# Where the stores of kept orders stand between the two stages of a transform-and-attention kernel

## The reference

```
coeff = complex(x[..., 0], x[..., 1]) * sqrt_eig
h = irfft(einsum('nlm,mlk->nkm', coeff, pct), n=512, norm='forward')   # 64 x 256 x 512
z = layernorm(h)
logits = tanh(einsum(z @ K, z) + bias) * temperature, within a band of 12 of 256 rows
h = h + softmax(logits) @ z
h = h + ffn(layernorm(h))      # seven small layers on the few rows whose two marks are set
```

## Time and profile before

| | |
|---|---|
| median of three executions | 1432.56 us (1427.76 to 1433.67) |
| profiled execution | 1427.68 us |
| its span, first to last instruction | 1425.8 us |
| TensorE busy | 1335.9 us, 94% |
| VectorE, ScalarE, GpSimd busy | 65%, 63%, 39% |
| granted TensorE clock, mean over the span | 0.981 |
| bytes moved by DMA | 219.71 MB, mean 154 GB/s |

### The profile page before, as it was taken

One profiled execution on the slowest core, in us unless ns is written; L12 is line 12 of the kernel. 1 busy time (PEld: TensorE's weight loads), 2 busy tenths in 40 slices (PEclk: granted clock), 3 DMA queues, 4 the chain that ended last, 5 costly groups with the idle time before them and its releaser, 6 DMA issues. The chain is left out here.

```text
span 1425.8 us, 30434 instructions
## 1 busy us (share of the span) xinstructions
PE 1335.9 (94%) x8813; PEld 1159.2 (81%) x8813; DVE 928.9 (65%) x2026; ACT 899.8 (63%) x1956; POOL 557.0 (39%) x1394
## 2 busy tenths in 40 slices
PE   6989788969899999999999999999999989999994
PEld 4767566759799999999999999999999989555551
DVE  1222222326687887878888788887888877767772
ACT  1222222325577777777777777777777767867772
POOL 0000000000355555555555555555555546622222
PEclk9999999999999999999999999999999999999997
DMA  9999999995563333333333333333333332100000
GB/s 375 423 423 424 425 426 424 424 361 162 177 152 76 95 86 82 95 78 96 86 82 87 81 99 86 82 85 83 100 80 87 86 102 48 47 12 9 9 4 5
DMA packets 88338, 219.71 MB, mean 154 GB/s; under 512 B 20805, under 2 KB 33745, under 8 KB 75921
## 3 DMA queue, kind: packets, MB, share of 16 engines
q1 hardware_dynamic: 78265, 194.70, 42.7%
q10 hardware_dynamic: 4648, 22.89, 3.9%
q0 software_dynamic: 5376, 1.52, 0.6%
HBM read 147.69 MB, written 72.68 MB: 155 GB/s over the span
## 5 line engine op out<-in xcount | busy, mean ns | idle before, releaser
L708 PE MATMUL ps_k<-sphi,Glo 128*128 128x256 f32 x1024 | 292.0, 285 | 0.0
L707 PE MATMUL ps_k<-splo,Ghi 128*128 128x256 f32 x1024 | 290.7, 284 | 0.0
L706 PE MATMUL ps_k<-sphi,Ghi 128*128 128x256 f32 x1024 | 288.4, 282 | 0.0
L276 PE MATMUL s1b<-pg,cg 128*128 128x256 f32 x1024 | 241.1, 394 | 36.0 <-DVE cg L246 35.8
L276 PEld LDWEIGHTS s1b<-pg,cg 128*128 128x128 f32 x1024 | 197.5, 196 | 82.1 <-DVE cg L246 30.1
L246 DVE TENSOR_TENSOR cg<-xg,se 128x1024 f32<-128x1024 f32 x63 | 77.2, 1225 | 218.3 <-DMA pg<-in_pct_dram 206.2
L1478 POOL TENSOR_SCALAR ve<-var 128x2 f32<-128x2 f32 x64 | 13.9, 217 | 473.6 <-ACT squares L1083 473.5
L706 PEld LDWEIGHTS ps_k<-sphi,Ghi 128*128 128x128 f32 x1024 | 194.5, 190 | 2.4
L707 PEld LDWEIGHTS ps_k<-splo,Ghi 128*128 128x128 f32 x1024 | 192.9, 188 | 2.7
L708 PEld LDWEIGHTS ps_k<-sphi,Glo 128*128 128x128 f32 x1024 | 193.5, 189 | 0.0
L1466 POOL DMA_INDIRECT recs<-rec,idx x128 | 137.7, 1075 | 54.7 <-issue 54.7
(11 more groups left out here) (176 smaller groups left out, 3134.4 us busy)
## 6 DMA issues: line engine op xcount, KB each, us to landing
pg<-in_pct_dram SPq DMA_DIRECT2D x63, 1024.0 KB, 13.0
out_dram<-o SPq DMA_DIRECT2D x64, 512.0 KB, 2.8
xg<-in_xs_dram SPq DMA_DIRECT2D x63, 512.0 KB, 10.4
xt<-spec SPq DMA_DIRECT2D x60, 512.0 KB, 5.2
spec<-stage ACTq DMA_DIRECT2D x42, 512.0 KB, 8.3
rrow<-rs SPq DMA_DIRECT2D x64, 128.0 KB, 4.5
spec<-hold SPq DMA_DIRECT2D x12, 480.0 KB, 6.0
spec<-apart SPq DMA_DIRECT2D x10, 512.0 KB, 11.6
```

Source lines behind the costliest of these rows:

```text
L276: last = nc.tensor.matmul(bank[at * PARTS + part][:, m % 2, :], cg[:, b % SETS, m * 2 + h, :], pg[:, b, m * 2 + h, :], start=(h == 0), sto ...
L706: nc.tensor.matmul(out_ap, whi, mhi, start=(j == 0), stop=False)
L707: nc.tensor.matmul(out_ap, whi, mlo, start=False, stop=False)
L708: last = nc.tensor.matmul(out_ap, wlo, mhi, start=False, stop=(j == n - 1))
```

## The change

The store of eight orders of `apart` becomes a helper, `store_apart`. Of the five pairs of stores, two pairs (j = 1 and 0) stay behind the last loads and count on a new semaphore, `rows_stored`; the three others (six stores) go to the head of the middle stage on the sync engine, ahead of its wait. The two `first_apart` pieces are issued by ScalarE both at group 55 (before: at groups 56 and 58). Five of the six `first_held` pieces are now issued by the sync engine behind the four stores, and the sixth by ScalarE after its last copy. VectorE waits for the four stores before h of item 0, and for the six before h of item 2.

```diff
--- before.py
+++ after.py
@@ -90,6 +90,7 @@
         self.x0_loaded = ctx.enter_context(nc.semaphore("x0_loaded"))
         self.hold_at = (nc.sbuf_base + 31) // 32 * 32
         self.hold = sb("hold", [P, HELD * GM, NLAT])
+        self.rows_stored = ctx.enter_context(nc.semaphore("rows_stored"))
         self.apart_stored = ctx.enter_context(nc.semaphore("apart_stored"))
         self.apart = nc.alloc_sbuf_tensor_at("apart", [P, APART * GM, NLAT], F32, offset=APART_AT)
 
@@ -104,6 +105,14 @@
         self.iota = sb("iota", [P, 16])
         self.Wf = sb("Wf", [P, MID, WCOLS])
         self.W1f = sb("W1f", [64, 4, P])
+
+
+def store_apart(eng, spec, const, j, stored):
+
+    m0 = NLAT - KEPT * GM + 8 * j
+    for c in range(2):
+        eng.dma_start(spec[0:NB, c * NLAT + m0:c * NLAT + m0 + 8, :],
+                      const.apart[c * NB:c * NB + NB, 8 * j:8 * j + 8, :]).then_inc(stored, 16)
 
 
 def stage1_spectrum(nc, const, xs_in, pct_in, se_in, K_in, FT_in, others, spec):
@@ -215,11 +224,12 @@
                     load_half(g, g % RING1, 1)
 
             sp.wait_ge(copied, (GROUPS - HELD) * PARTS)
-            m_apart = NLAT - KEPT * GM
-            for j in range(APART * GM // 8):
-                for c in range(2):
-                    sp.dma_start(spec[0:NB, c * NLAT + m_apart + 8 * j:c * NLAT + m_apart + 8 * j + 8, :],
-                                 const.apart[c * NB:c * NB + NB, 8 * j:8 * j + 8, :]).then_inc(const.apart_stored, 16)
+            for j in (1, 0):
+                store_apart(sp, spec, const, j, const.rows_stored)
+            for m0, m1 in ((0, (HELD - 2) * GM), ((HELD - 2) * GM, (HELD - 1) * GM), ((HELD - 1) * GM, HELD * GM)):
+                sp.wait_ge(copied, (GROUPS - HELD) * PARTS + m1 // 2)
+                for c in range(2 if m1 < HELD * GM else 1):
+                    first_held(sp, c, m0, m1)
 
         @block.vector
         def _(dve):
@@ -342,15 +352,10 @@
                     for c in range(2):
                         act.dma_start(spec[:, bass.ds(g * GM + (c * NLAT - GM), 2 * GM), :],
                                       stage[c * NB:(c + 1) * NB, half]).then_inc(stored[half], 16)
-                if isinstance(g, int) and g in (GROUPS - 8, GROUPS - 6):
+                if isinstance(g, int) and g == GROUPS - 9:
                     act.wait_ge(copied, (GROUPS - HELD) * PARTS)
-                    first_apart(act, (g - GROUPS + 8) // 2)
-                if isinstance(g, int) and g >= GROUPS - 3:
-                    m0, m1 = ((0, (HELD - 2) * GM), ((HELD - 2) * GM, (HELD - 1) * GM),
-                              ((HELD - 1) * GM, HELD * GM))[g - GROUPS + 3]
-                    act.wait_ge(copied, (GROUPS - HELD) * PARTS + m1 // 2)
                     for c in range(2):
-                        first_held(act, c, m0, m1)
+                        first_apart(act, c)
                 if lead and g in KF_AFTER:
                     c = KF_AFTER[g]
                     act.wait_ge(pe_KF, c + 1)
@@ -363,6 +368,8 @@
             for dst, src in others:
                 act.dma_start(dst, src).then_inc(const_loaded, 16)
             groups(nc.scalar, group)
+            act.wait_ge(copied, GROUPS * PARTS)
+            first_held(act, 1, (HELD - 1) * GM, HELD * GM)
             for half in range(2):
                 act.wait_ge(stored[half], 32 * ((GROUPS - KEPT + 2 - 2 * half) // 4))
 
@@ -620,7 +627,10 @@
                                  const.hold[c * NB + n:c * NB + n + 1, :, :].rearrange("o (p q) w -> o p (q w)", q=2)
                                  ).then_inc(x_loaded[n], 16)
 
-            sp.wait_ge(const.apart_stored, 16 * APART * GM // 4)
+            for j in range(2, APART * GM // 8):
+                store_apart(sp, spec, const, j, const.apart_stored)
+            sp.wait_ge(const.rows_stored, 64)
+            sp.wait_ge(const.apart_stored, 96)
             for n in range(1, 3):
                 load_first(n, FROM)
 
@@ -1315,7 +1325,9 @@
                     n, k1 = i + 1, (k + 1) % 4
                     dve.wait_ge(dve_eo, n * 4 + 4)
                     if isinstance(n, int) and n == 0:
-                        dve.wait_ge(const.apart_stored, 16 * APART * GM // 4)
+                        dve.wait_ge(const.rows_stored, 64)
+                    if isinstance(n, int) and n == 2:
+                        dve.wait_ge(const.apart_stored, 96)
                     wait(dve, act_hhi, n - 3)
                     wait(dve, act_var1, (n - 3) * 2)
                     hv = h[:, k1].rearrange("p t (s w) -> p t s w", s=2)
```

## The result

The changed kernel takes 1436.02 us in the median of 14 executions (1433.95 to 1439.83); the kernel before, timed beside it, 1429.70 (1426.05 to 1438.33). The ratio is 1.0040, 95% interval 1.0028 to 1.0052: 4 to 7.4 us slower. The ratio is inside the 0.5% that I called no change, the end of the interval just beyond it. The time lies in my range, near its upper end. My 0.5 us does not hold; the price lies above that of the slower rival.

What follows compares the result with a forecast made beforehand. Up to about 393 us sync's chain of rows, not TensorE, was taken to bound the kernel. Block 0's 4 us gain is waited off, leaving the chain's +0.5 on 1432.56, the median of three executions: 1433 us, range 1426.5 to 1436.5.

Steps and rivals of the forecast that it cites:

- My 0.5 us: Whole kernel: net cost of the change, +0.5 us, from the first rrow being asked for at 333.6 instead of 333.08.
- the slower rival: Middle stage's start: the six stores land late, after 326.3 and up to 327; +2.5 to +4 us, 1431; chance 0.27.
- My 1433: Whole kernel: forecast time in us, 1432.56 + 0.5 rounded.
- the gain at block 0 is waited off at block 1: Start of middle stage: block 0 starts 4.0 us earlier, but that and 0.4 more is lost waiting for block 1's load.
- my 2.6: End of block 0's gather: a transfer with nothing before it in the queues takes 2.6 us to land.
- Landed at 325.3, bounds 324.3 and 327: Head of sync's middle stage: six stores issued from 316.0 take 7.5 to 8.2 us of transfer at 422 GB/s.
- The ends of the chain's range: First rrow on sync's chain: -1.3 and +2.5 us, from the two ends of the stores' landing.
- Item 1's load, 4.5 us: Block 1's load, behind the six stores: 4.5 us to arrive, bounds 3.6 and 6.0, so there at 329.8.
- The clock: TensorE standing 3.1 us before block 1: clock drops to 1.2 GHz, transform takes 3.6 us instead of 1.95.
- The chain of rows: Sync after block 0: rs reached at 329.5, behind load data until 332.6; rrow asked for at 333.6, +0.5 us.
- TensorE's loss is taken up by its later holes: TensorE at 371 and 388: its +1.1 us vanishes in holes of 2.07 and 2.16 us, which end by the chain.
- The rival that block 0 starts no earlier: Block 0's gather: last piece needs 5 to 6 us regardless of stores, start only 1 us earlier; 1428.2; chance 0.08.

Runs made afterwards that it cites:

- two queues: Changed kernel, the six stores at the head of the middle stage issued half by sync, half by ScalarE; ratio 1.0038 against the kernel before.
- the stores alone: Changed kernel with only the stores moved; block 0's held pieces all issued by ScalarE as in the kernel before; ratio 1.0036.
- the pieces alone moved: Kernel before with all ten stores still behind the last loads; only block 0's held pieces go to sync, the last to ScalarE; ratio 1.0008.
- the padded kernel before: Kernel before the change, with items of spec in DRAM 4 KiB further apart; ratio 1.0004.
- the turned layout: spec with real and imaginary halves outermost, one store from 128 partitions; four kernels: changed 1.0006, before 0.9984, item 1 from the chip 0.9998, eight stay 0.9981.
- eight stores staying: Changed kernel, but eight stores stay behind the last loads and two move to the middle stage: ratio 0.9997; with 128-partition stores 0.9981.
- the one with 128-partition stores: Changed kernel with spec's halves outermost, so eight orders are one 1 MB store from all 128 partitions, three at the middle stage's head; ratio 1.0006.
- larger transfers: Changed kernel, its six 512 KB stores at the head of the middle stage made two of 1.5 MB; ratio 1.0060 against the kernel before.

## Why the prediction was right, and where it failed

- **The time inside the range**: in part luck. My 1433 stands on 1432.56, the median of three executions; the median of 14 of the kernel before is 1429.70. The change costs 6.3 us in the medians and not 0.5, and the lower base hid 2.9 of that.
- **That the gain at block 0 is waited off at block 1**: right. Predicted start 317.3, measured 315.90, with the first stage 0.7 us later than in the trace before (its last matmul ends at 313.19 instead of 312.50). The last piece took 2.0 us to land, below my 2.6.
- **"Landed at 325.3, bounds 324.3 and 327"**: the step that failed. The term was six stores in 7.5 to 8.2 us of transfer; they took 13.75 us from the first issue to the landing, where I had 9.3; they moved 175 GB/s in the first 3 us and 265 in the mean, not 422. I took the rate from the stretch 307 to 312, in which the stores stand behind loads, and did not ask which partitions they read. Read from all 128 partitions the same bytes land after 9.4 us. The lag then is near what I computed: item 1 at 331.15, first rrow at 334.44 (predicted 329.8 and 333.6, with the last matmul of the first stage at 313.91 instead of 312.50), and the whole is +0.6 us, my +0.5. That the whole agrees so well is partly chance: its interval goes from -0.7 to +2.4 us, and the layout may change the last stage too.
- **The ends of the chain's range**: mis-added. By the prediction's own steps a landing at 324.3 or 327 puts rrow at 332.6 or 335.3, so -0.5 and +2.2 us, where it has -1.3 and +2.5. It also prices its rivals from 1427.68 and its forecast from 1432.56.
- **The slower rival** named the mechanism, late stores, but priced it only up to 327, by slow issue; issue was not the cause, and the landing was beyond its end. It should have had the larger chance.
- **Item 1's load, 4.5 us**: 5.1 (329.26 to 334.35).
- **The clock**: right in kind. It fell in the stand, and the transform took 3.79 us (predicted 3.6).
- **The chain of rows**: of the 7.85 us by which sync is late at item 1's load, 4.0 reach the first rrow. Before, rs of item 0 had waited for rstd from 325.60 to 330.44; that slack of 4.8 us took up a part, and rs landing behind load data (3.5 us instead of 2.6) gave 0.8 back. This is the sum as I made it, with another number at its head.
- **TensorE's loss is taken up by its later holes**: not seen here. They were 2.07 and 2.16 us; the lag goes from 2.9 at item 3 to 4.9 at item 7. With two queues and with the stores alone, which land as late, it is 1.3 and 1.4 us at item 7, so single profiles don't settle it, and I have no experiment on this part.
- **The rival that block 0 starts no earlier**: fell, 315.90. The observation behind it was real: before, the last pieces on ScalarE's queue, issued by 316.16, are seen at 321.26, and with the ten stores gone a lone piece takes 2.0 us (313.84 to 315.88). The Trainium skill (DMA: Bandwidth & Descriptors, Queues, rings and completion order) says that a completion count lands only after every earlier write of its DMA engine. The trace before doesn't need that: after 320 ScalarE's queue still moves a packet of data and its count, so the data themselves came late, in turn with the stores on the same DMA engines. With the pieces alone moved, ScalarE's lone piece was through by 318, while stores ran until past that.

```profile
q10 hardware_dynamic: 2, 0.00, 0.4%
```

**Left open.** In the profile after, 3.0 us of the 9.3 between the spans are a stand of ScalarE in the last stage, at about 1370, released by nothing that the trace shows:

```profile
ACT act_f L959 <- remote: 3.0, 1, 3.0
```

The time from the last rrow to the end of the span is 216.8 us in the profile before and 221.5 after. Such a stand, 3.0 to 4.5 us long, is in every other profile of the old layout, the padded kernel before among them, and there this time is 220.9 to 223.9 us. It is in none of the four profiles of the turned layout, where the time is 215.0 to 215.8. So the profile before is the exception among those of its layout, and part of the 9.3 us between the two spans is the chance of one execution. Nothing that the change touches runs there. How the median's +6.3 us divides between the passage and the last stage, one profile of each kernel can't say. Nor is it shown that the turned layout wins its 2 to 3 us by the earlier first rrow: with eight stores staying, the eighth rrow is at 429.78 without it and 428.60 with it, 1.2 us apart, and the time behind the last rrow is 8.4 us shorter. Why the stand comes and goes I can't say.

## What to carry to other kernels

A transfer rate is a property of which partitions are read at the same time, not of the queue alone: here stores from 64 partitions moved 417 GB/s behind loads and right behind a barrier 175, rising to 295. When transfers are moved out of the way of one wait, ask what waits for them at their new place, and price them at the rate of a start from idle, read from a stretch like it. If both halves of a tensor go to DRAM, try a layout in which one transfer takes all 128 partitions. And before two versions are compared by one profile each, look at the stages that no edit touches: here they differ by more than the effect.

## What the runs showed of the hardware

- 64-partition stores behind a barrier: 175 GB/s in their first 3 us, 223 GB/s at 0.95 busy a little later, 295 from 320 to 328; 128-partition stores at the same place: 426 GB/s. 8 KB packets: 0.63 us in the first store, 0.31 with 128 partitions. The port figure of the Trainium skill (SBUF — State Buffer, Door 1: The DMA port swizzle), 218 GB/s for partitions 0 to 63, is near the rate at the start. The row pitch of 512 KiB costs copies between DRAM tensors little by the Trainium skill (DMA: Bandwidth & Descriptors, Latency and other measured facts); here a pad of 4 KiB changed nothing.
- Transfers of the two halves in flight together moved 417 GB/s behind the loads. The Trainium skill (SBUF — State Buffer, "Can I just issue two DMAs to hit both halves?") says that they don't add up, +6%. In the last row of rates here they did; behind the barrier they did not at first, and in part from 320 on.
- Two issuing queues and larger transfers brought nothing for stores from 64 partitions. The larger ones were slower (16.6 against 13.7 us); I take it that they keep the engines on one half for longer, and their rate did not rise with time:

```profile
318.00:322.00 4.00, 4.00 (x36) 4.00 (x36) 2.20 (x6) 1.52 (x4) 0.00 (x0) 1.00 0.98 197
322.00:326.00 4.00, 1.91 (x17) 1.70 (x15) 0.69 (x1) 0.66 (x3) 0.94 (x2) 1.00 0.81 197
```

- The same stand can leave the clock or lower it. In the changed kernel and in the one with 128-partition stores TensorE stood 2.37 us alike before its first transposes of the middle stage; then the granted clock was 0.50 from 316 to 319 in the one and 1.00 from 318 to 322 in the other, and block 0's transform took 3.63 and 2.05 us. What decides it, no run here shows.
